# A graph layer with slice attention on one core: how TensorE tells the other engines of its progress in the block loop, a ring of 32 slots, and slice weights kept in DRAM

## What is computed

```python
x = x + gnn(layernorm(x))          # support = x @ W; r = sigmoid(support @ a2); gated = r * support
                                   # out[row] = sum over edges of ew * gated[col] / sum of ew * r[col]
                                   # out = max(out,0) + softplus(out @ a1) * min(out,0); elu
x = x + ffn(layernorm(x))          # 8 heads of 64, 64 slices:
# slice_weights = softmax((x @ W_x @ W_slice + b) / temp)          [node, head, slice]
# slice_token   = sum over nodes of slice_weights * (x @ W_fx) / (sum of slice_weights)
# out_slice     = softmax(q k^T / 8) v   on the 64 slices of a head
# out           = sum over slices of slice_weights * out_slice, then @ W_out + b_out
```

## Time and profile before

| | us |
|---|---|
| median of 3 runs | 1673.46 (1667.9 to 1676.08) |
| the profiled execution | 1665.41 |
| its span, first to last instruction | 1663.6 |
| PE busy | 1253.5 (75%) |
| DVE busy | 1063.6 (64%) |
| POOL busy | 929.5 (56%) |
| ACT busy | 367.4 (22%) |

### The profile page before, as it was taken

How to read it: one execution, slowest core, us unless ns; L and a number is a source line. 1 busy time by engine, 2 the same in 40 slices (tenths; PEclk the granted TensorE clock), 3 DMA queues, 4 the chain that set the end, 5 groups by cost and what they waited for, 6 DMA issues and landing times.

```text
span 1663.6 us, 21782 instructions
## 1 busy us (share of the span) xinstructions
PE 1253.5 (75%) x6275; PEld 988.9 (59%) x6275; DVE 1063.6 (64%) x2767; ACT 367.4 (22%) x1224; POOL 929.5 (56%) x921
## 2 busy tenths in 40 slices
PE   3796676788888778786786766876668767787898
PEld 2686565677676667573554544654446545555787
DVE  8879777777776866344665565656566656665322
ACT  0442011110000000001232232323223322233232
POOL 0587766655665665556665656666666656661000
PEclk9898787877787788857888877887888888888999
DMA  7114343543443333534533333633333433341122
GB/s 236 47 67 66 92 120 108 117 118 105 112 118 108 107 109 110 114 70 116 105 98 101 101 100 102 109 97 105 102 105 106 105 99 106 105 111 29 36 76 72
DMA packets 164248, 166.74 MB, mean 100 GB/s; under 512 B 85171, under 2 KB 136391, under 8 KB 164140
## 3 DMA queue, kind: packets, MB, share of 16 engines
q0 software_dynamic: 40544, 108.37, 24.7%
q1 hardware_dynamic: 102428, 37.71, 9.4%
q10 hardware_dynamic: 21168, 19.35, 3.9%
HBM read 136.86 MB, written 28.49 MB: 99 GB/s over the span
## 4 chain that ended last, share of the span: by engine, by line
PE 39%; DVE 26%; another core or an unknown queue 16%; issue 13%; ACT 4%; DMA 1%; POOL 0%; DVEq 0%; SPq 0%; POOLq 0%; ACTq 0%
PE bank L1698 38%; DVE S L1290 3%; DVE big L967 3%; DVE big L937 2%; DVE S L1118 1%; DVE big L928 1%; DVE neg L1328 1%; ACT big L1640 1%; DVE lg L1316 1%; DVE hm L1311 1%; DVE ag L1301 1%; DVE big L921 1%; DVE big L952 1%; DVE big L945 1%
## 5 line engine op out<-in xcount | busy, mean ns | idle before, releaser
L834 POOL DMA_INDIRECT rows<-gated_rows_dram,ring_i x516 | 511.8, 992 | 295.1 <-issue 151.2
L1698 PE MATMUL bank<-rows,S 128*128 128x257 f32 (+1 forms) x2254 | 605.8, 408 | 79.4 <-issue 50.4
L1698 PEld LDWEIGHTS bank<-rows,S 128*128 128x128 f32 x2254 | 448.2, 205 | 204.7 <-issue 121.0
L736 POOL DMA_INDIRECT rows<-gated_rows_dram,lg x294 | 290.0, 986 | 194.1 <-PE bank L1698 95.7
L1698 PE MATMUL bank<-big 128*104 128x80 f32 (+3 forms) x1849 | 249.2, 302 | 99.5 <-DVE big L967 53.2
L1698 PEld LDWEIGHTS bank<-big 128*104 128x104 f32 (+2 forms) x1849 | 242.8, 219 | 112.1 <-issue 107.6
L1698 PE MATMUL bank<-Wxs,xT 128*128 128x512 f32 x196 | 150.2, 910 | 100.1 <-ACT xT L1627 99.9
L1290 DVE TENSOR_SCALAR S<-iota,lof,srec 128x128 f32<-128x128 f32 x588 | 165.4, 355 | 4.7 <-remote 4.5
L1301 DVE TENSOR_TENSOR ag<-bank,ovr 128x257 f32<-128x257 f32 x49 | 20.9, 427 | 206.5 <-remote 102.6
L1698 PEld LDWEIGHTS bank<-Wxs,xT 128*128 128x128 f32 x196 | 47.9, 270 | 155.2 <-ACT xT L1627 107.0
L1547 ACT COPY ovr<-bank 128x257 f32<-128x257 f32 x98 | 36.8, 375 | 335.2 <-PE bank L1698 276.1
(11 more groups left out here) (258 smaller groups left out, 1474.3 us busy)
## 6 DMA issues: line engine op xcount, KB each, us to landing
overflow_sums_dram<-ovr ACTq DMA_DIRECT2D x98, 128.5 KB
rows<-gated_rows_dram,ring_i POOLq DMA_INDIRECT x516
gated_rows_dram<-rows SPq DMA_DIRECT2D x49, 128.5 KB, 2.4
ovr<-overflow_sums_dram SPq DMA_DIRECT2D x49, 128.5 KB
rows<-gated_rows_dram SPq DMA_DIRECT2D x49, 128.5 KB
out_dram<-S SPq DMA_DIRECT2D x48, 128.0 KB, 1.7
rows<-gated_rows_dram,lg POOLq DMA_INDIRECT x294
res<-in_x_dram SPq DMA_DIRECT2D x1, 4352.0 KB
```

What stands on the lines that cost most here:

```text
L736: pool.indirect_dma_start(rows[:, turn(n), :], None, gtab[:, :], bass.IndirectOffsetOnAxis(ap=ring1[:, n:n + 1], axis=0)).then_inc(s_row[t ...
L834: pool.indirect_dma_start(rows[:, slot(b, u), :], None, gtab[:, :], bass.IndirectOffsetOnAxis(ap=ring_i[:, b // CH % 2, n:n + 1], axis=0)) ...
L1698: return nc.tensor.matmul(o, l, r, start=start, stop=stop, skip_group_check=True)
```

## The change

- `RING` becomes 32: the 16 new slots of rows and selection matrices lie in the big tile, in the part that held the sums of the first part and later `swt`. Two neighbouring slots share one semaphore, so TensorE waits for both of a pair. GpSimd and VectorE wait once for the new part to be free (`s_free`).
- Each attention step of the loop comes one or two blocks later: in block b TensorE does `turn_weights(b-5)` and `sums(b-5)`, `logits(b-3)` and `cross(b-2)`. Buffers for it: five of normalised rows (`XN`), three of logits (`lgs`), and bank 5 beside bank 7 for the turned weights.
- Inside the loop `crossed`, `largest`, `shift`, the normalisation's output and `keep` have no wait for TensorE of their own any more. What they read was done before the end of a block for which their engine has waited already (`take`, or ScalarE's wait ahead of `own`). The four marks stay: GpSimd's ring, `own` and `take` use them.
- `keep` writes into a buffer of two blocks (`swb`), and SyncE stores it to a new DRAM tensor (`store_sw`, 256 KB a block, each store issued when the one before has landed). In the output part ScalarE's queue loads the blocks back in pairs into four slots (`NST`), the first four pairs while the small steps run; TensorE's and ScalarE's output loops are written out. VectorE's and SyncE's stay hardware loops.
- After the loop five blocks of sums and three of logits are left rather than four and two, in a new order, with fewer filling matmuls (`spin`) between them.

The diff, cut to its core:

```diff
-RING = SL - 2
+OLD = SL - 2
+RING = 32
+XN = 5
+NST = 4
...
+        xn_more = [carve(F) for k in range(XN - 3)]
+        swb = carve(2 * HG).rearrange("p (k n) -> p k n", k=2)
+        lg_more = carve(HG)
+
+        carve = Carve(big, 0, NB * GW)
+        more_rows = carve((RING - OLD) * GW).rearrange("p (u w) -> p u w", w=GW)
+        more_S = carve((RING - OLD) * P).rearrange("p (u r) -> p u r", r=P)
+        carve = Carve(big, 0, NB * GW)
+        stg = carve(2 * NST * HG).rearrange("p (s k n) -> p s k n", s=NST, k=2)
 
         carve = Carve(rows_t, 0, RW)
...
+        def rows_at(b, u):
+            r = slot(b, u)
+            return more_rows[:, r - OLD, :] if u < TS and r >= OLD else rows[:, r, :]
+
+        def S_at(b, u):
+            r = slot(b, u)
+            return more_S[:, r - OLD, :] if u < TS and r >= OLD else S[:, r if u <= TS else SL, :]
+
+        def landing(b, u):
+            return s_row[slot(b, u) // 2]
...
-        def filled(b, u):
-            return (b * TS + u) // RING + 1 + (NT1 + SL - 1 - slot(b, u)) // SL
+        assert TS % 2 == 0 and RING == 2 * OLD
+
+        def score_bank(b):
+            return bank[0] if b == LAST - 1 else bank[4]
+
+        def turn_bank(b):
+            return bank[7 - b % 2 * 2]
+
+        def landed(b, u):
+            j = slot(b, u) // 2
+            return (NT1 + SL - 1 - j) // SL + 2 * ((b * TS + u) // RING + 1)
 
         MARKS = (3, 7, TS, TQ - 1)
...
-        def after(b, lag, mark, own):
-            return (s_seg, done(b + lag, mark)) if b + lag <= LAST else (own, b + lag - LAST)
-
-        def turned_over(b):
-            return after(b, 2, MARKS[0], s_rt)
-
-        def scored(b):
-            return after(b, 2, MARKS[1], s_lm)
-
-        def summed(b):
-            return after(b, 4, MARKS[0], s_M)
...
+            def store_sw(b):
+                sp.wait_ge(s_wc, b + 1)
+                if b:
+                    sp.wait_ge(s_sd, 16 * b)
+                sp.dma_start(swd[b, :, :], swb[:, b % 2, :]).then_inc(s_sd, 16)
...
+                if b >= XN + 2:
+                    store_sw(b - (XN + 2))
...
+            for b in range(LAST - 4, NB):
+                store_sw(b)
...
+                    if b * TS + u == OLD:
+                        pool.wait_ge(s_free, 1)
+                        pool.sem_inc(s_tick, 1)
                     if freed(b, u) > seen[0]:
                         seen[0] = freed(b, u)
                         pool.wait_ge(s_seg, seen[0])
                         pool.sem_inc(s_tick, 1)
-                    tile(u, s_row[slot(b, u)])
+                    tile(u, landing(b, u))
...
             def largest(b):
-                dve.wait_ge(*scored(b))
-                step(v.tensor_reduce(hm[:, 0, :], heads(bank[4][:, :]), AX.X, ALU.max))
+                if b > LAST - 3:
+                    dve.wait_ge(s_lm, b - (LAST - 3))
+                step(v.tensor_reduce(hm[:, 0, :], scores(b), AX.X, ALU.max))
 
             def shift(b):
-                if b >= 2:
-                    dve.wait_ge(*summed(b - 2))
-                v.tensor_tensor(heads(lg[:, b % 2, :]), heads(bank[4][:, :]),
+                if b > LAST - 2:
+                    dve.wait_ge(s_M, b - (LAST - 2))
+                v.tensor_tensor(heads(lgs[b % 3]), scores(b),
                                 hm[:, 0, :].unsqueeze(2).broadcast_to([P, H, G]), ALU.subtract).then_inc(s_ls, 1)
...
-                if b:
-                    crossed(b - 1)
                 if b >= 2:
-                    expo(b - 2)
+                    crossed(b - 2)
+                if b >= 3:
+                    expo(b - 3)
                 step.n = 2
                 step.loop = b
                 guess(b + 1, col(RS), col(LV), col(VA))
                 act.wait_ge(s_rs, b + 1)
-                if b >= 3:
-                    act.wait_ge(*summed(b - 3))
-                a.activation(xn[:, b % 3, :], res[:, b, :], ACT.Identity,
+                a.activation(xns[b % XN], res[:, b, :], ACT.Identity,
                              bias=col(NM), scale=col(RS)).then_inc(s_xn, 1)
-                if b >= 3:
-                    keep(b - 3)
+                if XN <= b < LAST:
+                    keep(b - XN)
...
             def crossed(b):
-                act.wait_ge(*turned_over(b))
-                if b:
-                    act.wait_ge(*scored(b - 1))
+                if b > LAST - 2:
+                    act.wait_ge(s_rt, b - (LAST - 2))
+                    act.wait_ge(s_lm, b - (LAST - 2))
...
             def keep(b):
+                if b > LAST - 5:
+                    act.wait_ge(s_M, b - (LAST - 5))
+                if b >= 2:
+                    act.wait_ge(s_sd, 16 * (b - 1))
                 n = P if b < LAST else TAIL
-                act.wait_ge(*summed(b))
+                o = swb[:, b % 2, :].rearrange("p (c n) -> p c n", n=P)
+                t = turn_bank(b)[:, :].rearrange("p (c n) -> p c n", n=P)
                 if n < P:
-                    a.copy(swt[:, :, b * P + n:(b + 1) * P],
-                           bank[7][:, :].rearrange("p (c n) -> p c n", n=P)[:, :, n:P])
+                    a.copy(o[:, :, n:P], t[:, :, n:P])
                 for c in range(NP2):
-                    m = a.activation(swt[:, c, b * P:b * P + n], bank[7][:, c * P:c * P + n], ACT.Identity, bias=zcol[:, 0:1],
+                    m = a.activation(o[:, c, 0:n], t[:, c, 0:n], ACT.Identity, bias=zcol[:, 0:1],
                                      accum_out=nacc[:, c, b:b + 1])
                 m.then_inc(s_wc, 1)
...
+            def load(i):
+                n = len(blocks(i))
+                if i >= NST:
+                    act.wait_ge(s_o, 2 * (i - NST) + 2)
+                act.wait_ge(s_sd, 16 * (2 * i + n))
+                act.dma_start(stg[:, i % NST, 0:n, :], swd[2 * i:2 * i + n, :, :].rearrange("b p n -> p b n")).then_inc(s_wl[i % NST], 16)
+
+            for i in range(NST):
+                load(i)
...
-            for b in range(LAST):
-                segment(b + 1, 0, 1)
+            for b in range(1, NB):
+                segment(b, 0, 3)
+                if b >= XN:
+                    turn_weights(b - XN)
+                    sums(b - XN, 0, 2)
+                segment(b, 3, 6)
+                if b >= XN:
+                    sums(b - XN, 2)
+                segment(b, 6, 8)
+                own(b)
                 if b >= 3:
-                    turn_weights(b - 3)
-                segment(b + 1, 1, 2)
-                if b >= 3:
-                    sums(b - 3, 0, 2)
-                segment(b + 1, 2, 3)
-                if b >= 3:
-                    sums(b - 3, 2)
-                if b:
-                    cross(b - 1)
-                segment(b + 1, 3, 7)
-                if b:
-                    logits(b - 1)
-                segment(b + 1, 7, 8)
-                own(b + 1)
-                segment(b + 1, 8, TQ)
+                    logits(b - 3)
+                segment(b, 8, 9)
+                if b >= 2:
+                    cross(b - 2)
+                segment(b, 9, TQ)
+            pe.wait_ge(s_ev, LAST)
+            turn_weights(LAST - 4)
+            sums(LAST - 4)
+            cross(LAST - 1)
+            logits(LAST - 2)
+            spin(6, 1)
+            cross(LAST)
+            pe.wait_ge(s_ev, NB)
+            logits(LAST - 1)
             turn_weights(LAST - 3)
             sums(LAST - 3)
-            cross(LAST - 1)
-            logits(LAST - 1)
+            logits(LAST)
             turn_weights(LAST - 2)
             sums(LAST - 2)
-            spin(12, 5)
-            cross(LAST)
-            logits(LAST)
-            spin(6, 5)
             turn_weights(LAST - 1)
...
-            def product(b, k, first):
-                pe.wait_ge(s_wl, b + 1)
-                if not first:
+            def product(b):
+                k = b % 2
+                i = b // 2
+                if k == 0:
+                    pe.wait_ge(s_wl[i % NST], 16 * (i // NST + 1))
+                if b >= 2:
                     pe.wait_ge(s_os, b - 1)
                 for c in range(NP2):
-                    m = mm(bank[4 + k][:, 0:F], stg[:, k, c * P:(c + 1) * P], Pm[:, c, :], c == 0, c == NP2 - 1)
+                    m = mm(bank[4 + k][:, 0:F], stg[:, i % NST, k, c * P:(c + 1) * P], Pm[:, c, :], c == 0, c == NP2 - 1)
                 m.then_inc(s_o, 1)
 
-            product(0, 0, True)
-            product(1, 1, True)
-            with pe.Fori(1, NB // 2) as i:
-                for k in range(2):
-                    product(i * 2 + k, k, False)
-            product(LAST, 0, False)
+            for b in range(NB):
+                product(b)
```

124 lines of the change are left out of this document (65 added, 59 removed).

## The result

The changed kernel is slower: 1779.22 us median (1769.09 to 1798.78) against 1671.46, ratio 1.0649 [1.0594, 1.0704]. I had forecast 1626 and a range to 1705. The profiled execution took 1774.91 us, its span is 1772.6.

The account below looks back on a forecast made before the run. The prediction took waits in the block loop, from TensorE signals late beside unbroken gathers, as the bound. -58 + 10 + 1 = -47 gave 1618 against the profiled execution, 1626 as median; range 1560 to 1705.

Parts of the forecast that it names:

- What bounds the kernel: Block loop: no engine full, waits bind; TensorE's signals come 3 to 11 us late after some 9 us of unbroken gathers.
- GpSimd's account: Block loop's 772 us: 498 gathers at 1.26 (627), pauses 113, 13 behind the last gather, some 20 of smaller things.
- Ring of 32: GpSimd's gathers in the block loop: pauses at the ring nearly end, 57 to 113 us go, the lower end taken.
- No mid-block wait: Block loop: TensorE's 99.9 us for xT go; blocks take 14.9 us instead of 16.1, 58 us, the ring's same gain.
- L: Lateness with which a block's predecessor's end is seen, 6 to 11 us; such a block takes L + 8.6.
- The +10 for a deeper lead at the end: Behind the last gather TensorE has two to three blocks left instead of one: 10 to 20 us given back, 10 taken.
- Stores at 0: Stores to DRAM in the block loop, 256 KB a block: contention costs between 0 and 10 us, 0 taken.
- pairs at 0: Slot pairs on one semaphore: TensorE waits up to 1.26 us more only where caught up with GpSimd, hidden in the lead.
- After the loop +1: Stretch after the block loop: more sums and logits, less filling, late stores; between -4 and +6 us, +1 taken.
- Output loop 0: Output loop stays PE-bound at 1.73 us a block and its loads keep up; between 0 and +87 us, 0 taken.
- the slower one: Rival for the block loop: the deeper ring makes signals later; centre 1715, to 1760 us, chance 0.19.
- GpSimd's pace: Rival for the block loop: all 113 us of pauses go, 20 given back at the end; 1580 us, chance 0.22.

Follow-up runs that it names:

- the small program: Reference's computation left out: rounds of TensorE and VectorE beside GpSimd's gathers, plain transfers or multiplications; 626.23 us with late signals, 549.9 to 551.2 with prompt ones.
- the lead of 16: Changed kernel with gathers waiting for the tile 16 before, not 32: ratio to before 0.9871 with late signals (1653.50 us), 1.0039 to 1.0072 with prompt ones.
- the prompt condition: Sets of runs with signals on time: kernel before 1419 to 1432 us (late: 1663 to 1682); unedited changed kernel there 1430.43, ratio 1.0049.
- the prompt run: Small program of rounds beside 48 gathers, with eight ways of breaking the stream; rounds 2.63 us, kernel before at 1430.10.

## Why the prediction was wrong, point by point

*What bounds the kernel.* The late marks and the link to GpSimd's streams, read from the earlier trace rows, were right; the small program shows them by themselves. Its onset is 12 us of unbroken gathers, where I had read some 9. Not seen, and not to be seen from one trace: it is a condition, without which the same kernel takes 1425.

*GpSimd's account.* 1.26 us a gather and 627 us for 498 held in every run.

*Ring of 32: the step that failed.* "What goes is between 27 x 2.1 = 57 us and all 113." The waits went from 128.6 to 232.6 us. I took a pause's length as fixed and its number as what the ring decides, so the term was a gain of 57 us, where the lead of 32 by itself costs 8% of the time. Pauses did fall, from 53 to 28, but their length hangs on the backlog that a stream leaves: 25 us behind 39 us of gathers. The ring was what kept streams short.

*No mid-block wait.* The wait went. My block of 14.9 us hung on ends 6 to 11 us late; with the ring of 32 they came up to 38 late and the mean was 18.35. The form was roughly right and the L wrong: in the worst place L is 38 (due about 785, seen at 823.17), which gives 10.3 + 38 + 8.6 = 57 us for two blocks, and the trace has 50.2 + 12.1 = 62. With the lead of 16 the mean was 15.84, a loop shorter by 12 us where this step had -58: too large even by itself, because `take` still waits up to 15.6 us for such ends. The +10 for a deeper lead at the end was +4: 16.8 us from the last gather to the last `take` in place of 12.9. By the block account it should not have stood there at all, as -58 covers the loop up to the last `take`.

*Stores at 0, pairs at 0:* with all else of the change, 0.5% in the prompt condition; neither was measured apart in the late one. *After the loop +1:* +0.5. *Output loop 0:* +4.6. Its loads kept up, at 182 GB/s, but the output's stores land later beside them (2.7 us in place of 1.7) and there are two buffers for them. That does not account for all of it: in the prompt condition they land as late (2.6), VectorE waits 40.9 us for them, and the loop is longer by 0.5 alone. Ten traces with the new output loop give 83.3 to 89.3 us for these steps, in either condition (the two of before 82.9), so 4.6 is one draw of an added cost that scatters, and why it does is open.

*The rivals.* What happened is the slower one by its own mechanism, to which I gave 0.19. Its size was short (1715 to 1760 against 1779): it had half of the blocks at 19.7 us, the trace has ten `take`s 29 to 50 us behind the one before. Its argument "for" named the stretch with the worst lateness and the 40 us that 32 slots allow. The argument "against", that a late end stops TensorE and the ring then fills and pauses by itself, is true, but filling 32 slots takes those 40 us. The sign to look for, 40 us stretches of gathers, was there; VectorE's steps at 1 us throughout were not: the trace names 24 waits of 0.96 to 1.29 us of VectorE on its own steps, in 8 of the 49 blocks, where it named 6 before. GpSimd's pace, the rival at 1580, is what holds in the prompt condition, where it leaves nothing to gain.

## What to carry to other kernels

A buffer that sometimes makes an engine wait can be what paces another resource; before deepening it, ask what the pauses let through, and price a pause by the work piled up ahead of it, not by its present mean. If a signal is seen microseconds after its cause, find what runs beside it and measure that alone, in more than one set of runs: 17% of this kernel's time hangs on it, and a gain that holds in one condition can be nothing or a loss in the other. A lead of one block (10 tiles) was already enough where signals were prompt, so 32 had nothing to win.

## What the runs showed of the hardware that I had not expected

The same program took 1425 or 1672 us, in whole sets of runs, on two of the chips both; what sets the condition is open. In the late one, a round trip between TensorE and VectorE grows from 2.63 to 20 us after 12 us of unbroken gathers, even of 32 B pieces, and not beside plain transfers from the same engine (the round of 20 has 1.8 us of a lower granted clock in it). The Trainium skill ("DMA: Bandwidth & Descriptors", the section on SWDGE, HWDGE and iDMA) puts both kinds of GpSimd's transfers on one path, whose software writes descriptors into rings in SBUF. By that alone both should disturb alike; the runs differ, with rounds of up to 20.3 us against 2.63.

TensorE itself crawls late in a long stream: in the changed kernel single matmuls come 2.1 to 2.8 us apart between 794 and 802, and again between 924 and 932, there in `sums`, where no matmul waits for a signal between them. They last 0.46 to 0.59 us, at a granted clock of 0.50 in the first stretch, and the engine is idle for 1 to 3.1 us before each; why is open. And in the prompt run a landing wait for the third-last gather of a stream cost 0.6 us at most, where one for the last cost 2.5 to 4.8.
